# Two-layer graph network: half of each quad's first layer norm computed on ScalarE instead of VectorE

## What is computed

```python
def _layernorm(x, axis=-1, eps=1e-05):
    m = jnp.mean(x, axis=axis, keepdims=True)
    v = jnp.var(x, axis=axis, keepdims=True)
    return (x - m) / jnp.sqrt(v + eps)

def _L1_gnn_ref(feat, fc_weight, attn, eps, src, dst):
    proj = feat @ fc_weight.T
    el = proj[src]
    er = proj[dst]
    e = jnp.sum(jax.nn.leaky_relu(el + er, NEG_SLOPE) * a, axis=-1)
    gate = jax.nn.sigmoid(jnp.sum(el * er, axis=-1))
    w = jax.nn.sigmoid(e * gate)
    msg = feat[src] * w[:, None]
    neigh_sum = jax.ops.segment_sum(msg, dst, num_segments=N)
    neigh = neigh_sum / jnp.maximum(deg, 1.0)[:, None]
    return (1.0 + eps[0]) * feat + neigh

x = _layernorm(x + _L0_gnn_ref(x, edge_index, edge_type_9, ...), axis=-1)   # gated recurrent unit
x = _layernorm(x + _L1_gnn_ref(x, fc_weight, attn, eps, src, dst), axis=-1)
```

## Time and profile before

| | us |
|---|---|
| median of three runs | 3239.43 |
| lowest and highest | 3234.38, 3239.57 |
| the profiled execution, whole | 3231.14 |
| its span, first to last instruction | 3229.2 |
| TensorE busy | 2138.5 (66%) |
| VectorE busy | 2498.1 (77%) |
| ScalarE busy | 1622.6 (50%) |
| POOL busy | 2116.6 (66%) |
| granted TensorE clock, mean | 0.771 |
| stage of the change, about | 1066 to 1128 |

### The profile page before, as it was taken

How to read it: one execution, slowest core, us unless ns; L and a number is a source line. 1 busy time by engine, 2 the same in 40 slices (tenths; PEclk the granted TensorE clock), 3 DMA queues, 4 the chain that set the end, 5 groups by cost and what they waited for, 6 DMA issues and landing times. The chain is left out here.

```text
span 3229.2 us, 64872 instructions
## 1 busy us (share of the span) xinstructions
PE 2138.5 (66%) x13842; PEld 1729.5 (54%) x13842; DVE 2498.1 (77%) x12793; ACT 1622.6 (50%) x3531; POOL 2116.6 (66%) x2179
## 2 busy tenths in 40 slices
PE   1499999999989545556555555555556565555654
PEld 1377777777754445455455555544545454454554
DVE  6677777777726678788888888878888888888887
ACT  2365655555533365455455454544544454554455
POOL 2436667667640077777777777777777777777772
PEclk9999999999989776675666666666666767766665
DMA  7212222222230565655655555555555556556553
GB/s 146 84 37 71 70 69 72 67 69 71 69 86 0 167 175 159 169 162 158 169 164 160 163 167 163 157 168 164 159 166 164 161 158 170 164 155 168 164 160 103
DMA packets 357885, 425.07 MB, mean 132 GB/s; under 512 B 174163, under 2 KB 242141, under 8 KB 357740
## 3 DMA queue, kind: packets, MB, share of 16 engines
q0 software_dynamic: 103728, 266.13, 29.7%
q1 hardware_dynamic: 251800, 156.64, 18.6%
q10 hardware_dynamic: 2212, 0.60, 0.1%
HBM read 399.44 MB, written 23.70 MB: 131 GB/s over the span
## 5 line engine op out<-in xcount | busy, mean ns | idle before, releaser
L1430 POOL DMA_INDIRECT got<-rows,idx x1624 | 1545.7, 952 | 547.7 <-issue 518.7
L1599 PE MATMUL sum_ps<-whot,got 128*128 128x128 f32 x3264 | 690.6, 381 | 639.7 <-DVE whot L1442 566.6
L1599 PEld LDWEIGHTS sum_ps<-whot,got 128*128 128x128 f32 x3264 | 593.9, 273 | 728.4 <-DVE whot L1442 636.2
L742 POOL DMA_INDIRECT got<-x_rows,idx x532 | 534.1, 1004 | 283.1 <-issue 161.1
L1592 PE MATMUL er_ps<-win,hot_t 128*128 128x128 bf16 x4932 | 531.1, 286 | 271.5 <-ACT hot_t L1540 239.8
L1498 DVE CUSTOM_DVE_ANT_0 small_rows<-got,er_ps 128x128 f32<-128x128 f32 x1624 | 370.0, 283 | 355.4 <-DMA got<-rows,idx 348.1
L897 ACT CAST work<-c_ps 128x318 bf16<-128x318 f32 x1092 | 455.3, 430 | 376.5 <-PE c_ps L973 368.2
L1592 PEld LDWEIGHTS er_ps<-win,hot_t 128*128 128x128 bf16 x4932 | 472.6, 134 | 313.6 <-ACT hot_t L1540 268.8
L924 PE MATMUL span_ps<-x_parts,work 128*126 128x393 bf16 x2756 | 610.0, 331 | 0.0
L1442 DVE TENSOR_SCALAR whot<-iota_f,dl,w_s 128x128 f32<-128x128 f32 x1632 | 463.1, 360 | 0.3 <-ACT w_s L1545 0.3
L1573 ACT ACTIVATE small_rows<-er_ps 128x512 f32<-128x512 f32 x406 | 242.4, 597 | 370.3 <-DVE er_ps L1510 368.3
(11 more groups left out here) (240 smaller groups left out, 1792.2 us busy)
## 6 DMA issues: line engine op xcount, KB each, us to landing
work<-dst_row SPq DMA_DIRECT2D x413, 256.0 KB, 3.9
got<-rows,idx POOLq DMA_INDIRECT x1624
win<-parts SPq DMA_DIRECT2D x118, 96.0 KB
got<-x_rows,idx POOLq DMA_INDIRECT x532
idx<-src_rows SPq DMA_DIRECT2D x413, 2.0 KB, 3.5
parts<-split SPq DMA_DIRECT2D x13, 384.0 KB, 4.2
x_rows<-x_parts SPq DMA_DIRECT2D x2, 2320.5 KB
rows<-nodes SPq DMA_DIRECT2D x13, 256.0 KB, 2.6
```

What stands on the lines that cost most here:

```text
L742: pool.indirect_dma_start(got[:, c, i, 0:3 * D], None, x_rows, bass.IndirectOffsetOnAxis(ap=idx[:, c, i:i + 1], axis=0)).then_inc(gathered ...
L1430: pool.indirect_dma_start(got[:, c, i, :], None, rows, bass.IndirectOffsetOnAxis(ap=idx1[:, c, i:i + 1], axis=0)).then_inc(gathered[c], 16)
L1599: mm = pe.matmul(sum_ps[:, 0:P], got[:, c, i, D:2 * D], whot[:, c, i, :], start=(c == 0 and i == 0), stop=(c == NS - 1 and i == STEP - 1))
```

## The change

The last two tiles of each quad are normalised on ScalarE, as Identity(rstd * x + shift), with a new vector shift = -mean * rstd, computed for all 52 tiles on VectorE at the end of the gates block. ScalarE does quad 0 ahead of its loop and quad q + 1 at the top of the call for quad q. TensorE and SP wait for both parts. Two semaphores of the statistics become one.

```diff
@@ gates block
-            aggr_done = sem("aggr_done")
@@ VectorE, stats_of
                         if q:
-                            dve.wait_ge(aggr_done, QUAD * q)
+                            dve.wait_ge(stats_done, 2 * QUAD * q)
                         for i in range(QUAD):
                             dve.bn_stats(stats[:, i, :], nodes[:, q * QUAD + i, :]).then_inc(stats_done, 1)
                         for i in range(QUAD):
-                            dve.wait_ge(stats_done, QUAD * q + i + 1)
-                            dve.bn_aggr(moments[:, q * QUAD + i, :], stats[:, i, :]).then_inc(aggr_done, 1)
+                            dve.wait_ge(stats_done, 2 * QUAD * q + i + 1)
+                            dve.bn_aggr(moments[:, q * QUAD + i, :], stats[:, i, :]).then_inc(stats_done, 1)
@@ VectorE, end of the gates block
-                    dve.reciprocal(rstd[:], rstd[:])
+                    dve.reciprocal(rstd[:], rstd[:]).then_inc(spread, 1)
+                    dve.wait_ge(spread, 3)
+                    dve.scalar_tensor_tensor(out=shift[:], in0=moments[:, :, 0], scalar=-1.0, in1=rstd[:],
+                                             op0=ALU.mult, op1=ALU.mult)
@@ norm and projection block
+            normed_act = sem("normed_act")
+            HERE = QUAD // 2
+            assert NQ % 2
@@ VectorE
-                            for t in range(q * QUAD, (q + 1) * QUAD):
+                            for t in range(q * QUAD, q * QUAD + HERE):
@@ TensorE, ahead of the transposes of quad q
-                        pe.wait_ge(normed, QUAD * q + QUAD)
+                        pe.wait_ge(normed, HERE * q + HERE)
+                        pe.wait_ge(normed_act, (QUAD - HERE) * (q + 1))
@@ ScalarE
+                    def normalise(q):
+                        for i in range(HERE, QUAD):
+                            t = bass.ds(q * QUAD + i, 1)
+                            act.activation(nodes[:, t, :].rearrange("p t f -> p (t f)"),
+                                           nodes[:, t, :].rearrange("p t f -> p (t f)"), ACT.Identity,
+                                           scale=rstd[:, t], bias=shift[:, t]).then_inc(normed_act, 1)
+
                     def copy_quad(h, b):
                         q = h * 2 + b
+                        if not isinstance(q, int) or q + 1 < NQ:
+                            normalise(q + 1)
                         act.wait_ge(f_turned, q + 1)
...
+                    normalise(0)
                     each_quad(act, copy_quad)
@@ SP, ahead of the store of nodes
-                        sp.wait_ge(normed, QUAD * q + QUAD)
+                        sp.wait_ge(normed, HERE * q + HERE)
+                        sp.wait_ge(normed_act, (QUAD - HERE) * (q + 1))
```

More of the change, by code:

```diff
@@ L134, in graph_layers @@
         rstd = sb("rstd", [NODES, NTL], F32)
+        shift = sb("shift", [NODES, NTL], F32)
         dl = sb("dl", [P, GROUP], F32)
@@ L1147, in _ @@
                         stats_of(q)
-                    dve.wait_ge(aggr_done, NTL)
+                    dve.wait_ge(stats_done, 2 * NTL)
                     dve.tensor_scalar(rstd[:], moments[:, :, 1], LN_EPS, None, ALU.add).then_inc(spread, 1)
                     dve.wait_ge(spread, 2)
-                    dve.reciprocal(rstd[:], rstd[:])
+                    dve.reciprocal(rstd[:], rstd[:]).then_inc(spread, 1)
+                    dve.wait_ge(spread, 3)
+                    dve.scalar_tensor_tensor(out=shift[:], in0=moments[:, :, 0], scalar=-1.0, in1=rstd[:],
+                                             op0=ALU.mult, op1=ALU.mult)
         def each_quad(eng, quad):
```

## The result

The changed kernel took 3246.94 us (median of seven runs, 3241.69 to 3257.39), the one before 3234.98 us beside it (3233.58 to 3239.57). The ratio is 1.0040 with an interval of 1.0029 to 1.0051: slower by 9.4 to 16.5 us, 12 by the medians. The profiled execution took 3246.94 us, its span is 3245.1.

A forecast was written before the change was run, and what follows sets the result against it. ScalarE's loop was taken as the bound in one part, TensorE in the other. Loop 5.95, start 0.15 and clock 0.5 summed to 6.6 us, added to 3239.4 for 3246.0 us; range 3237.5 to 3253.

The forecast's parts named there:

- ScalarE's loop as the bound: In the stage, norms ahead of f_s lengthen ScalarE's loop to 3.69 us, over TensorE's 3.17, so it sets every step.
- Quads 3 and 4: Steps into quads 3 and 4 grow from 2.92 to 3.69 us, 1.54 us together.
- Quad 1: Step from quad 0 to 1 grows by 0.77 us, because norm(2) stands before f_s(1).
- Quads 5 to 11 without the clock: Seven steps grow from TensorE's 3.17 to 3.69 us, 3.64 us together at the high clock.
- Quad 2: Step from quad 1 to 2 costs 0: norm(3) fits into the 2.36 us wait for TensorE's 13 transposes of dst_f.
- Start and shift vector: Before quad 0, new shift instruction and ScalarE's first norm cost net +0.15 us, between -0.25 and +0.8 with a late fetch.
- Register operations at 0: The sequencer's register work stays hidden on ScalarE, 0 us; exposed, it would add up to 6.6 us, chance 0.10.
- The clock: TensorE dropping to 1.2 GHz in quads 2 to 5: 0.5 us in the sum, bounds 0 and 5; as rival, chance 0.12.
- Where the delay goes: In the tail, the 13 split stores start 0.78 us behind the last proj store and move with quad 12; delay arrives whole.
- rival 4: VectorE is the stage's true bound, so each quad gives back 0.51 us, 6.7 in all: 3232.7 us, chance 0.03.

The follow-up runs named there:

- the order without the gaps: Changed kernel with f_s of the next quad ahead of the split copy and the norm in the wait: ratio 0.9994; with degree counts also spread, 0.9969.
- the last run: Kernel before, all tiles on VectorE, with f_s of the next quad ahead of the split copy on ScalarE: ratio 1.0017, stage 55.2 us.

## Why the prediction was right, and where it was not

The direction and the loop through ScalarE were right, the size was not: +6.6 us forecast, +12 measured, with 9.4 at the lower end of the interval. That 3246.0 lies beside 3246.9 is two errors that cancel: the median it was counted from, 3239.4, came out 4.4 us lower over seven runs, and the change 5.4 us higher. That the absolute time fits is luck.

Point by point, in the profiled stage:
- *ScalarE's loop as the bound*: right. 3.65 to 3.67 us where the clock stays, forecast as 3.69, up to quad 11; 2.81 in quad 12. Moving the norm behind f_s takes the cost away.
- *Quads 3 and 4*: +1.54 forecast, +1.50 measured. *Quad 1*: +0.77, measured +0.75. *Quads 5 to 11 without the clock*: +3.64, measured 7 x (3.66 - 3.17) = 3.43.
- *Quad 2*: 0 forecast, -0.49 measured. The clock rose earlier relative to TensorE's work: the 13 transposes of dst_f ended 0.13 us sooner, and the quad's own four took 0.60 us instead of 0.97.
- *Start and shift vector*: +0.15, measured +0.12. VectorE's first norm starts 1.03 us behind the reciprocal (1069.31 to 1070.34) instead of 0.78 (1065.61 to 1066.39), 0.25 later where 0.26 was estimated, and ScalarE's first norm starts 0.11 us behind VectorE's (1070.45), where the prediction has "some 0.1" from no row. The late fetch of its upper bound shows in no run.
- *Register operations at 0*: right. Between split copy, norms and f_s ScalarE shows no idle time in the changed kernel (1089.00, 1089.48, 1090.26), and three tiles show none either. By count there are 42 in twelve calls, 3.5 a call, not six, and with three tiles 66, 5.5 a call. One took 35 to 99 ns, where the upper bound had 0.1 us.
- *The clock*: this is the step that failed. "I put 0.5 in the sum as its weight", within 0 to 5 us, and placed it in quads 2 to 5. In the changed kernel's two profiles the falls came in quads 6 and 11; in the first they cost 7.67 - 3.43 = 4.24 us. A low step with degrees took 2.1 us more than a high one, where the bound had about 2.9 from no row. I had counted the 0.5 us of TensorE's new gap in each step with degrees as room to spare, and looked for danger only in the thin quads 3 and 4, on the ground of gaps above 2 us in the second layer. That danger is real too, only not in these two profiles: with three tiles, with the gaps filled from quad 5 on and with the counts moved, the clock fell in quads 3 and 4. With the gaps filled from quad 3 on it stayed up (53.17 us), and so it did in equally long steps without a gap (50.82 us). The views name the two levels only as granted 1.00 and 0.50; the 2.4 and 1.2 GHz of the prediction stand in none of them. What they show of the levels is the time: eight passes of the projection took 1.16 us at the upper and 2.08 at the lower one.
- *Where the delay goes*: right; stores 0.78 us behind, 14.15 us long.
- *VectorE as the bound*, rival 4: refuted by the run with the norm in the wait.

Sum of the measured terms: 0.12 + 0.75 - 0.49 + 1.50 + 3.43 + 4.24 = 9.55 us, the stage's growth. It lies at the lower end of the interval; the medians' further 2.4 us have no cause shown.

## What to carry to other kernels

An engine's idle time can be used only where it stands: work handed to a half-idle engine belongs behind the instruction whose answer it waits for, not ahead of it, and the order of time shows which side that is (stage 48.09 us behind it, 57.44 ahead of it). Before work is moved off the busiest engine of a stage, follow the loop through all engines; here VectorE was nearly full and yet idle for 0.27 us a step. Where the new bound opens gaps on a TensorE that was full, count the clock as a cost of its own (4.24 us here). Giving TensorE something to do held the clock only where every gap from the first thin quad on was filled (stage 53.17 us), and the loop's own cost stayed (5.3 us with the start); with the later gaps alone filled, one fall ahead of them cost more than before (74.8 us). The better cure is the order without the gaps (43.94 us with the counts spread, 47.4 without).

## What the runs showed of the hardware that I had not expected

- With gaps of 0.42 us in steps of 3.66 us, TensorE busy 12.44 of 13.70 us, and none longer since the clock had risen, the granted clock fell from 1.00 to 0.50 for 6.8 us (the changed kernel's second fall). Without gaps, in steps of 3.62 us of which passes of one column take 2.1, it stayed at 1.00 to the end of the work.
- Once low, it came back after 6.8 us of full work in the changed kernel, after 17.1 us (15.8 busy) in the last run, and after 51.2 us (49.3 busy) in the run filled from quad 5 on; with the degree counts moved it came back after 10.3 us of which TensorE was busy for 6.3. These runs do not tell why.
- With all tiles on VectorE the stage took 47.94 us on a chip on which the whole kernel took 4247 us, against 47.89 in the kernel before on one on which it took 3235. Why the whole differs these runs do not tell.
